# A gated delta layer on one core: the block inverse as three chained products in halves, key squares on ScalarE, values activated on their way out of PSUM

## What is computed

```python
        yc = jax.nn.silu(yc).transpose(0, 2, 1)          # causal convolution, 4 taps, then Silu
        q = q * jax.lax.rsqrt(jnp.sum(q * q, -1, keepdims=True) + L2_EPS)
        k = k * jax.lax.rsqrt(jnp.sum(k * k, -1, keepdims=True) + L2_EPS)
        def step(S, xs):
            qt, kt, vt, gt, bt = xs
            S = S * jnp.exp(gt)[..., None, None]
            kv = jnp.einsum('bhk,bhkv->bhv', kt, S)
            delta = (vt - kv) * bt[..., None]
            S = S + jnp.einsum('bhk,bhv->bhkv', kt, delta)
            o = jnp.einsum('bhk,bhkv->bhv', qt * scale, S)
            return (S, o)
```

## Time and profile before

| | us |
|---|---|
| timed, median of 3 | 2643.74 |
| timed, lowest and highest | 2641.07, 2652.4 |
| span of the profiled execution | 2649.7 |
| PE, DVE, ACT, POOL busy in the span | 2198.2, 1812.2, 1414.4, 338.8 |
| convolution steps on VectorE (L1595), 192 | 232.5 |
| projection of the delta layer on PE (L1196), 512 records | 230.0 |
| squares of the keys on GpSimd (L1160), 16 | 144.3 |

### The profile page before, as it was taken

How to read it: one execution, slowest core, us unless ns; L and a number is a source line. 1 busy time by engine, 2 the same in 40 slices (tenths; PEclk the granted TensorE clock), 3 DMA queues, 4 the chain that set the end, 5 groups by cost and what they waited for, 6 DMA issues and landing times. The chain is left out here.

```text
span 2649.7 us, 45005 instructions
## 1 busy us (share of the span) xinstructions
PE 2198.2 (83%) x18407; PEld 1693.0 (64%) x18448; DVE 1812.2 (68%) x3147; ACT 1414.4 (53%) x2265; POOL 338.8 (13%) x164
## 2 busy tenths in 40 slices
PE   7986387999999999999851797999999756887855
PEld 4665355777777777777740457999998533555633
...
DMA packets 159234, 122.23 MB, mean 46 GB/s; under 512 B 117712, under 2 KB 144976, under 8 KB 152528
## 3 DMA queue, kind: packets, MB, share of 16 engines
...
...
## 5 line engine op out<-in xcount | busy, mean ns | idle before, releaser
L1595 DVE SCALAR_TENSOR_TENSOR ctx_chan<-l1a_raw,l1a_cw,ctx_chan 128x1024 f32<-128x1024 f32 x192 | 232.5, 1286 | 20.1 <-ACT ctx_chan L1438 19.1
L1196 PE MATMUL banks<-x_chan,l1a_wp 128*128 128x512 f32 x512 | 230.0, 603 | 5.3 <-DMA l1a_wp<-in_l1a_wp_dram 5.3
L1160 POOL TENSOR_TENSOR l1a_sq<-ctx_chan 128x1024 f32<-128x1024 f32 x16 | 144.3, 9019 | 360.4 <-ACT ctx_chan L1442 360.4
L1196 PEld LDWEIGHTS banks<-x_chan,l1a_wp 128*128 128x128 f32 x512 | 97.8, 194 | 117.0 <-issue 110.6
L2723 PE MATMUL banks<-x_chan,more_weights_ahead 128*128 (+1 forms) x1024 | 121.1, 277 | 2.1 <-ACT l2a_ready L2579 2.1
L2723 PEld LDWEIGHTS banks<-x_chan,more_weights_ahead 128*128 128x128 f32 x1024 | 119.5, 194 | 3.8 <-issue 1.6
L1233 PE MATMUL banks<-l1a_wo,l1a_oT 128*128 128x256 f32 x512 | 121.2, 385 | 0.0
L1181 POOL TENSOR_TENSOR l1a_al<-l1a_aT,l1a_outer 128x1024 f32<-128x1024 f32 x32 | 74.8, 2358 | 323.9 <-DVE l1a_aT L1655 323.9
L1204 PE MATMUL banks<-l1a_wz,x_chan 128*128 128x256 f32 x512 | 115.5, 385 | 0.0
L2743 PE MATMUL banks<-l2a_wo,l2a_oT 128*128 128x256 f32 x512 | 113.2, 379 | 0.0
L1204 PEld LDWEIGHTS banks<-l1a_wz,x_chan 128*128 128x128 f32 x512 | 98.9, 194 | 19.8 <-issue 6.7
...
## 6 DMA issues: line engine op xcount, KB each, us to landing
...
```

The source lines that it names most:

```text
L1160: P.tensor_tensor(sq[:, 0, :], conv[:, 0, :], conv[:, 0, :], ALU.mult).then_inc(s["k_squared"], 1)
L1196: mm = MM(ps[:, 2 * (u % 2) + q, :], wp[:, c, u * 128:(u + 1) * 128], g.xT[:, c, t0:t0 + 512], start=c == 0, stop=c == 1)
L1595: V.scalar_tensor_tensor(t, raw[:, u, :, j:j + S], cw[:, c, j:j + 1], t, ALU.mult, ALU.add).then_inc(s["conv_done" if step == 2 else "conv ...
```

## The change

Four things, all in `layer1_delta`:

- The transposed E, E^2 and `p2` are gone. PE computes E (in two halves of eight slots), `xT1` = (1 + E) applied to `xT0`, `wT` = E applied to `xT1`, and E applied to `wT`; VectorE adds `xT1` to the last product and writes it as `xT2` (into the memory of `p1`). Each of the four products goes in two halves, with a semaphore each. ScalarE copies E, `xT1` and `wT` by halves.
- A half (`slot_half`) has both matmuls of a pair in the same bank, in partitions 0 to 63 and 64 to 127.
- Both squares are made by ScalarE in one operation of 2048 columns; GpSimd has none. On PE the sums stand before `xT1`; on ScalarE the Ln stands before the copy of `xT1`, the Exp behind the copies of `wT`. On VectorE one `add` moves between the convolution steps, and `p1` in front of the last of them.
- The values are no longer activated in place; the copy out of PSUM (`vt`) is a Silu.

The diff, its core:

```diff
-        x0, xT0, ec, ecT, p1, p2 = (L.sb(n, [128, VH, 64]) for n in "x0 xT0 ec ecT p1 p2".split())
-        xT1, xT2 = ecT, ec
+        x0, xT0, ec, p1, xT1, wT = (L.sb(n, [128, VH, 64]) for n in "x0 xT0 ec p1 xT1 wT".split())
+        xT2 = p1
...
+        def half_out(n, h):
+            return ps[:, 2 * n + h, :].rearrange("p (k n) -> p k n", n=64)
...
-            def square_keys(i):
-                if i:
-                    pool.wait_ge(s["kq_normed"], 2 * i)
-                pool.wait_ge(s["silu"], 4 * i + 1)
-                P.tensor_tensor(sq[:, 0, :], conv[:, 0, :], conv[:, 0, :], ALU.mult).then_inc(s["k_squared"], 1)
...
-            def both_halves(bank, lhsT, rhs):
+            def slot_half(bank, h, lhsT, rhs):
 
                 for row in range(2):
-                    for k in range(HALF):
+                    for k in range(HALF * h, HALF * h + 4):
                         tile64(bank, lhsT, rhs, k, row)
-                        mm = tile64(bank, lhsT, rhs, HALF + k, 1 - row)
+                        mm = tile64(bank, lhsT, rhs, k + 4, 1 - row)
                 return mm
...
-                pe.wait_ge(s["xT2_out"], i + 1)
+                pe.wait_ge(s["xT2_out"], 2 * i + 1)
                 for q in range(2):
                     for k in range(4):
                         mm = upper(q, k)
                     mm.then_inc(s["u_made"], 1)
+                pe.wait_ge(s["xT2_out"], 2 * i + 2)
...
-                    pe.wait_ge(s["silu"], 4 * i + 4)
+                    pe.wait_ge(s["conv_done"], 4 * i + 4)
...
-                both_halves(4, diagonal(al), within(x0)).then_inc(s["e1_made"], 1)
-                both_halves(6, within(x0), diagonal(al)).then_inc(s["e1T_made"], 1)
-                previous_out(1, 0, 2)
-                pe.wait_ge(s["e1T_out"], i + 1)
-                pe.wait_ge(s["e1_out"], i + 1)
-                both_halves(4, within(ecT), within(ec)).then_inc(s["e2_made"], 1)
+                for h in range(2):
+                    slot_half(4, h, diagonal(al), within(x0)).then_inc(s["e1_made"], 1)
+                previous_out(1)
+                next_sums()
                 pe.wait_ge(s["p1_made"], i + 1)
                 pe.wait_ge(s["xT0_in"], 128 * i + 128)
-                both_halves(6, within(p1), within(xT0)).then_inc(s["xT1_made"], 1)
-                next_sums()
-                pe.wait_ge(s["p2_made"], i + 1)
-                pe.wait_ge(s["xT1_out"], i + 1)
-                both_halves(4, within(p2), within(xT1)).then_inc(s["xT2_made"], 1)
-                previous_out(1, 2, 4)
+                for h in range(2):
+                    slot_half(6, h, within(p1), within(xT0)).then_inc(s["xT1_made"], 1)
+                for h in range(2):
+                    pe.wait_ge(s["e1_out"], 2 * i + h + 1)
+                    pe.wait_ge(s["xT1_out"], 2 * i + h + 1)
+                    slot_half(4, h, within(ec), within(xT1)).then_inc(s["wT_made"], 1)
+                for h in range(2):
+                    pe.wait_ge(s["wT_out"], 2 * i + h + 1)
+                    slot_half(6, h, within(ec), within(wT)).then_inc(s["xT2_made"], 1)
                 solve(i)
...
-            def square_queries(i):
+            def squares(i):
                 if i:
                     act.wait_ge(s["kq_normed"], 2 * i)
-                act.wait_ge(s["silu"], 4 * i + 2)
-                A(sq[:, 1, :], conv[:, 1, :], ACT.Square).then_inc(s["q_squared"], 1)
+                act.wait_ge(s["silu"], 2 * i + 2)
+                A(sq[:], conv[:, 0:2, :], ACT.Square).then_inc(s["squared"], 1)
...
-                    A(heads(vt, h), slots(h), ACT.Copy).then_inc(s["v_out"], 1)
+                    A(heads(vt, h), slots(h), ACT.Silu).then_inc(s["v_out"], 1)
...
-                act.wait_ge(s["e1_made"], i + 1)
-                A(ec[:], compact(2), ACT.Copy).then_inc(s["e1_out"], 1)
-                act.wait_ge(s["e1T_made"], i + 1)
-                A(ecT[:], compact(3), ACT.Copy).then_inc(s["e1T_out"], 1)
+                for h in range(2):
+                    act.wait_ge(s["e1_made"], 2 * i + h + 1)
+                    A(heads(ec, h), half_out(2, h), ACT.Copy).then_inc(s["e1_out"], 1)
                 if i == 0:
                     for u in range(2):
                         silu(1, u)
                 if more:
-                    square_queries(i + 1)
-                    for u in range(2, 4):
-                        silu(i + 1, u)
-                act.wait_ge(s["xT1_made"], i + 1)
-                A(xT1[:], compact(3), ACT.Copy).then_inc(s["xT1_out"], 1)
+                    squares(i + 1)
+                    norm_ln(i + 1)
+                for h in range(2):
+                    act.wait_ge(s["xT1_made"], 2 * i + h + 1)
+                    A(heads(xT1, h), half_out(3, h), ACT.Copy).then_inc(s["xT1_out"], 1)
+                for h in range(2):
+                    act.wait_ge(s["wT_made"], 2 * i + h + 1)
+                    A(heads(wT, h), half_out(2, h), ACT.Copy).then_inc(s["wT_out"], 1)
                 if more:
-                    norm_ln(i + 1)
                     norm_rs(i + 1)
-                act.wait_ge(s["xT2_made"], i + 1)
-                A(xT2[:], compact(2), ACT.Copy).then_inc(s["xT2_out"], 1)
...
-                    for first in (0, 2) if i else (0,):
-                        for step in range(3):
-                            convolve(i + 1, first, step)
-                v.wait_ge(s["e1_out"], i + 1)
+                    for step in range(3):
+                        convolve(i + 1, 0, step)
+                if i:
+                    if more:
+                        convolve(i + 1, 2, 0)
+                    add(i - 1, 0)
+                    if more:
+                        convolve(i + 1, 2, 1)
+                v.wait_ge(s["e1_out"], 2 * i + 2)
                 V.tensor_tensor(p1[:], ec[:], bc(fold[:], 1, VH), ALU.add).then_inc(s["p1_made"], 1)
-                if i:
-                    add(i - 1, 0)
-                else:
-                    for step in range(3):
-                        convolve(1, 2, step)
-                v.wait_ge(s["e2_made"], i + 1)
-                V.tensor_tensor(p2[:], compact(2), bc(fold[:], 1, VH), ALU.add).then_inc(s["p2_made"], 1)
                 if more:
+                    if i == 0:
+                        for step in range(2):
+                            convolve(1, 2, step)
+                    convolve(i + 1, 2, 2)
                     for h in range(2):
                         weigh(i + 1, h)
+                for h in range(2):
+                    v.wait_ge(s["xT2_made"], 2 * i + h + 1)
+                    V.tensor_tensor(heads(xT2, h), half_out(3, h), heads(xT1, h), ALU.add).then_inc(s["xT2_out"], 1)
                 if i:
```

41 lines of the change are left out of this document (16 added, 25 removed).

## The result

The changed kernel takes 2587.65 us, median of four runs (2587.01 to 2589.24); the kernel before, on the same chip, 2642.84 (four runs, 2641.07 to 2652.4). The ratio is 0.9778, 95% interval 0.9759 to 0.9796: 2.2% faster, 55 us. The forecast was 2587.

The account below looks back on a forecast made before the run. TensorE's own list bounds the kernel. 15 rounds x (3.3 - 0.4 - 0.15) = 41 us, first round 2.5, clock 12.9: total 57 off the median 2643.74 gives 2587 (own range 2575 to 2600; bounds 2574 to 2617).

Parts of the forecast that it names:

- The bound: Delta layer's rounds: TensorE, busy 58.6 of 61 us, is the bound; shortening its own list shortens the kernel; VectorE next.
- The stretch from the first product to the solve: TensorE in each round: 15.73 us falls to 12.4, saving 3.3 by one product, both waits and the seams.
- New gaps, 0.4 us a round: Three chained products in halves: waits for half copies cost nothing to 1.2 us a round; 0.4 taken.
- Late norms, 0.15 us a round: Norms' Exp behind wT's copies ends 0.85 us behind the solve's start; costs 0 to 1.1 us a round, 0.15 taken.
- The clock, 12.9 us: TensorE's clock falls behind the 0.76 us gap before the solve: nine falls of 1.43 us go with it.
- First round, 2.5 us: Layer's first round: longer square delays by 0.95 us, but the solve comes 2.5 us earlier net.
- VectorE: VectorE's queue: p1 ends at 722.6, ready 0.2 us before TensorE reaches xT1 at 722.85.
- Rival (b): VectorE becomes the bound, p1 and xT2's adds late by 1 to 2 us a round: 2610; chance 0.28 shared with (a).
- GpSimd: Key square takes 10.03 us on GpSimd, too late for the new order; moving it to ScalarE allows that order; no gain counted.
- Rival (a): Clock falls stay or half steps cost 0.2 us each: 32 us saved, 2612; chance 0.28 shared with (b).
- Rival (d): Before the first product, a DMA of the small blocks hides TensorE's new order: no gain, 2644; chance 0.03.
- Rival (c): Paired matmuls writing one bank run one after the other, 3.9 us a product: 62 us slower, 2706; chance 0.09.

Follow-up runs that it names:

- e4: Changed kernel, but each step of the chain (wT, last product, solve) waits for both halves of the one before; 2628.47 us, one run.
- e9: Kernel before, with only the last product, its copy and the solve's wait cut into halves and the norms' Exp behind the copy; 2627.57 us, ratio 0.9934.
- e3: Changed kernel, but the solve waits for both halves of xT2, which puts a gap back before it; 2608.76 us, ratio 0.9842 to the kernel before.
- e10: e6 with VectorE's add of the projected output moved behind p1 and all convolution steps; 2682.54 us, one run.
- e1: Kernel before, unchanged, profiled in another execution to count the clock falls again; 2646.5 us, span 2644.7.
- e7: Changed kernel, with the gated output turned into banks 4 to 7, without waiting for ScalarE's reading of banks 0 to 3; 2585.55 us.
- e6: Changed kernel, but GpSimd squares the keys again and TensorE's sums wait for both engines; 2589.69 us, one run.

## Why the prediction was right, point by point

**The bound.** Right: TensorE's own list. It got 3.26 us shorter in each round, and so did the round.

**The stretch from the first product to the solve.** Forecast 12.4 us without gaps, measured 12.41. The product's price of 1.94 held (1.88 to 1.95), and the projection in one piece (3.65 start to start, forecast 3.6) with the sums (0.99, forecast 1.0).

**New gaps, 0.4 us a round.** Too pessimistic: 0. Half 0 was reckoned to come back after 1.85 to 1.9 us and to be wanted at 1.94, level with no slack, and it came in time in every middle round. e4 shows what hung on it: 2.7 us a round.

**Late norms, 0.15 us a round.** The Exp is as late as forecast (it ends 0.86 behind the solve, forecast 0.85), but the trip through memory is shorter: from there to VectorE's scaling it takes 7.25 us, where 8.3 to 9.5 were taken over from before. VectorE waits 1.51 for it, TensorE not at all. Together these two terms were 8 us too large.

**The clock, 12.9 us.** Mechanism right in the main, size taken from the wrong thing. All falls of the middle rounds are gone, and e9 and e3 show with the same products that they nearly all go, and come back, with the gap; e9's first interval and e10 show that other waits bring them too. The prediction named the gap in front of nine falls, but not that six rounds had the same gap and no fall. And the nine were counted in one execution, with a span (2649.7) above the median time (2643.74), and then taken from the median, as if every execution had nine. Profiled against profiled the saving is 63.5; median against median 55. These 8 us made the forecast too optimistic, and they cancelled the 8 of the two terms above. That they are falls is likely, since e1 had three fewer with a span 5 us shorter, but nobody counted them in the other executions. That the time came out at 2587 to within 1 us is luck to that extent: two errors of 8 us with opposite signs.

**First round, 2.5 us.** Measured 3.15. The longer square took 1.91 us, and the first product came 0.7 later from the layer's first matmul (forecast 0.95).

**VectorE.** `p1` was forecast to be ready 0.2 us before it is wanted, and it was 0.33. Rival (b) did not happen, but it was the next in line: e7 took 1.4 us of waits away from elsewhere, and `p1` was late at once.

**GpSimd.** The step that failed. "It would have been late in the new order (sums at 721.8): the move to ScalarE is what allows that order" was read from a duration of 10.03 us, as if it were the square's own. In e6 the square in the new order takes 4.11 us and is in time in every middle round. Only in the first round is it late, as the sentence has it: TensorE waits 13.34 us for it. So the move to ScalarE does not make the order possible; by this one run it is worth 7.8 us in the layer, 6 of them in the first round. The error did not reach the forecast, because the sum has no term for the move. "VectorE lost nothing" holds for the twelve steps of the earlier trace rows, and for the part of the square in which GpSimd waits; as soon as the square gets on, VectorE loses 0.5 us (e6) or 1.6 (e10) if it has an operation with two operands in SBUF. This is the direction of what the Trainium skill says (SBUF — State Buffer, "Who interferes with whom"), by which one of the two engines blocks; the rows here show in addition that the one that is blocked can be held through some seven operations in a row, each of which starts after its own start is recorded (from 715.48 to 723.67 at 1.2 us each).

**Rival (a), falls or half steps stay.** Did not happen. **Rival (d), a DMA hides it.** Did not happen; the products start without a wait. **Rival (c), two row halves in one bank.** Refuted: such products took 1.88 to 1.95 us, those into two banks 1.91 to 1.97, and serialised ones would have taken 3.9. The rule of the Trainium skill (TensorEngine Tiling (Array Packing), "Gotcha 1: PSUM Pressure") that different row tiles cannot access the same bank at once differs here from the measurement, and the measurement decides: with the two in different partitions of the bank, as here, it costs nothing.
